# A graph network's first layer: every third block of nodes summed from rows gathered edge by edge

## What is computed

```python
h = jnp.maximum(_layernorm(x, axis=-1), 0.0)
msg = edge_val[:, None] * x[edge_src]          # x is h here, edge_val the edges' weights
neighbor = jax.ops.segment_sum(msg, edge_dst, num_segments=N_NODES)
out = neighbor @ W1.T + b1 + (x * neighbor) @ W2.T + b2
```

## Time and profile before

| | us |
|---|---|
| median of 3 runs | 2559.74 (2558.43 to 2564.2) |
| the profiled execution | 2558.8 |
| its span (first to last instruction) | 2556.4 |
| PE busy, and share of the span | 2265.3 (89%) |
| DVE busy | 1554.3 (61%) |
| ACT busy | 1235.4 (48%) |
| POOL busy | 133.9 (5%) |
| DMA, mean | 117 GB/s |

### The profile page before, as it was taken

The page is one execution under the profiler, slowest core; times in us unless marked ns, Lnnn a source line. Parts: engine busy times, 40 slices in busy tenths (PEclk is TensorE's granted clock), DMA queues, the critical chain, the costliest instruction groups (busy, mean ns, idle before and its releaser), DMA issues.

```text
span 2556.4 us, 58105 instructions
## 1 busy us (share of the span) xinstructions
PE 2265.3 (89%) x20263; PEld 2023.6 (79%) x20263; DVE 1554.3 (61%) x2760; ACT 1235.4 (48%) x3085; POOL 133.9 (5%) x114
## 2 busy tenths in 40 slices
PE   1599999999999999999987799999998426999897
PEld 1399999999999999999965566676787415888644
DVE  7677777777777777777745455555774582000133
ACT  4555555555555555555411577766886410000142
POOL 5300000000000000000000000000000340000000
PEclk7699999999999999999955899999999757999999
DMA  8222122112212212211233533233583147888221
GB/s 249 58 77 75 50 75 75 63 63 75 75 50 75 75 50 75 75 57 69 76 100 87 179 110 109 109 109 110 211 314 127 58 115 292 301 300 301 90 67 55
DMA packets 178788, 299.34 MB, mean 117 GB/s; under 512 B 13064, under 2 KB 130059, under 8 KB 178627
## 3 DMA queue, kind: packets, MB, share of 16 engines
q1 hardware_dynamic: 174592, 284.33, 32.2%
q0 software_dynamic: 4144, 14.34, 2.0%
HBM read 198.15 MB, written 100.49 MB: 117 GB/s over the span
## 4 chain that ended last, share of the span: by engine, by line
PE 82%; DVE 8%; DVEq 3%; issue 2%; ACT 2%; DMA 2%; ACTq 0%; POOLq 0%; POOL 0%; SPq 0%; PEldq 0%
PE ps L730 21%; PE ps L790 20%; PE ps L719 16%; PE ps L713 8%; PE ps L774 5%; PE ps L829 4%; PE ps L760 3%; PE ps L923 2%; DVE hT_s L1358 1%; DMA hs<-node_rows 1%; PE ps L820 1%; DVE carry L1554 1%; PE ps L837 1%; PE ps L960 0%; ACT edge_area L1010 0%
## 5 line engine op out<-in xcount | busy, mean ns | idle before, releaser
L1057 ACT CAST edge_area<-ps 128x392 f16<-128x392 f32 x784 | 385.5, 492 | 490.0 <-PE ps L713 490.0
L790 PE MATMUL ps<-big,rows_area 128*128 128x256 f16 (+1 forms) x4900 | 553.1, 274 | 24.8 <-DMA big<-edge_counts 24.8
L730 PE MATMUL ps<-big,rows_area 128*128 128x128 f32 x4802 | 571.3, 276 | 0.0
L730 PEld LDWEIGHTS ps<-big,rows_area 128*128 128x128 f32 x4802 | 550.9, 192 | 0.0
L719 PE MATMUL ps<-edge_area 128*128 128x196 f16 x4704 | 541.7, 250 | 0.0
L790 PEld LDWEIGHTS ps<-big,rows_area 128*128 128x128 f16 x4900 | 474.9, 99 | 82.8 <-DMA big<-edge_counts 25.1
L719 PEld LDWEIGHTS ps<-edge_area 128*128 128x128 f16 x4704 | 422.1, 97 | 0.3
L1063 ACT COPY big<-ps 128x392 f32<-128x392 f32 x784 | 384.5, 490 | 9.8 <-PE ps L719 1.4
L713 PE MATMUL ps<-edge_area 128*128 128x196 f16 x2352 | 334.4, 250 | 13.7 <-DVEq L1500 13.7
L1495 DVE TENSOR_TENSOR edge_area<-lo_pair,carry 128x768 f16<-128x768 f16 x392 | 218.7, 558 | 202.5 <-PE ps L719 124.1
L1496 DVE TENSOR_TENSOR edge_area<-cell_pair,carry 128x1176 f16<-128x1176 f16 x392 | 299.3, 764 | 0.0
(11 more groups left out here) (221 smaller groups left out, 1607.4 us busy)
## 6 DMA issues: line engine op xcount, KB each, us to landing
big<-edge_counts SPq DMA_DIRECT2D x336, 448.0 KB, 4.9
edge_counts<-edge_area SPq DMA_DIRECT2D x49, 1568.0 KB, 5.7
hs<-node_rows POOLq DMA_DIRECT2D x21, 448.0 KB, 4.5
x_stream<-edge_area SPq DMA_DIRECT2D x14, 448.0 KB, 3.9
node_rows<-edge_area SPq DMA_DIRECT2D x14, 448.0 KB, 3.0
edge_area<-x_stream SPq DMA_DIRECT2D x14, 448.0 KB, 3.9
node_rows<-rows_area SPq DMA_DIRECT2D x1, 3136.0 KB, 12.5
edge_area<-in_x SPq DMA_DIRECT2D x7, 448.0 KB, 4.7
```

What stands on the lines that cost most here:

```text
L730: last = mm(p_sum[par], h0[:, n, :], w32[:, par, n, :], start=(n == 0), stop=(n == NB - 1))
L790: last = mm(p_block[par][:, 0:width, :], planes[:, p, sh, :], piece[:, par, k, 0:width, j, :], start=(sh == 0 and p == 0), stop=(sh == NB ...
L1057: nc.scalar.copy(store_slot[:, par, :, cols], p_count[s % 2]).then_inc(sem("count_taken"), 1)
```

## The change

The halves are taken in sets of three (`SETS` = 16, and one half alone at the start). Of each set (in the code a `window(t)` with halves 3t+1, 3t+2 and 3t+3) two halves are done as before. The middle one, 3t+2, gets its counts but no weight matrix. Its sum is made edge by edge: its edges, at most 4608, lie as 36 columns (`SPAN`) of 128. For each column POOL gathers the 128 rows of h that the edges come from, from `node_rows` in HBM (64 KB), DVE makes an fp32 one-hot of the destination times the weight (`edge_onehots`), and PE multiplies the two, one fp32 matmul of 128x128 (`add_edges`), all 36 into one PSUM bank.

Three columns are a burst, and each set has 12 bursts: one is placed behind every fourth supergroup. Gathered rows have 12 buffers (`AHEAD` = 4 bursts), the one-hots 6 (`MADE` = 2 bursts). POOL also loads the next set's edge records (`load_set`), which DVE splits into indices and destinations (`split_set`, six small operations). The two remaining weight matrices' 98 matmuls are dealt over all 12 places, 8 or 9 each. The two PSUM banks of `weigh`'s sums become one for them and one for the edges. Loops now run over two sets on PE, ACT, DVE and POOL. A few small operations ahead of the stage work out where each set's records start; the general path for unsorted or too uneven input is taken too if a set has over 4608 edges.

```diff
+SETS = NHALF // 3
+SPAN = 36
+BURST = 3
+BURSTS = SPAN // BURST
+AHEAD = 4
+MADE = 2
...
+            def gather_set(t, q):
+                pool.wait_ge(sem("set_split"), t + 1)
+                for burst in range(BURSTS):
...
+                    pool.wait_ge(sem("edges_summed"), t * BURSTS + burst + 1)
...
+                    for n in range(BURST):
+                        c = burst * BURST + n
+                        pool.indirect_dma_start(
+                            out=edge_row[c % (AHEAD * BURST)], out_offset=None, in_=rows_dram,
+                            in_offset=bass.IndirectOffsetOnAxis(ap=set_idx[:, q, c:c + 1], axis=0),
+                        ).then_inc(sem(f"rows_in{burst % AHEAD}"), 16)
+                    if burst == AHEAD + 1:
...
+                        load_set(t + 1, 1 - q)
...
+            def add_edges(t, burst):
+                pe.wait_ge(sem(f"rows_in{burst % AHEAD}"), (t * (BURSTS // AHEAD) + burst // AHEAD + 1) * (16 * BURST))
...
+                pe.wait_ge(sem("edge_onehots"), t * BURSTS + burst + 1)
+                for n in range(BURST):
+                    c = burst * BURST + n
+                    last = mm(p_edges, edge_row[c % (AHEAD * BURST)], edge_oh[c % (MADE * BURST)],
+                              start=(c == 0), stop=(c == SPAN - 1))
+                last.then_inc(sem("edges_summed"), 1)
...
-            def duo_onehots(duo, slot):
-
-                dve.wait_ge(sem("weight_ready"), duo * 2 + 2)
+            def duo_onehots(duo, slot, weighted=True):
...
-                V.tensor_tensor(oh_whi[:, slot], oh_src[:, slot], whi.to_broadcast([P, 3, P, 2]), ALU.mult)
-                V.tensor_tensor(oh_wlo[:, slot], oh_src[:, slot], wlo.to_broadcast([P, 3, P, 2]), ALU.mult)
-                dve.drain()
+                if weighted:
+                    V.tensor_tensor(oh_whi[:, slot], oh_src[:, slot], whi.to_broadcast([P, 3, P, 2]), ALU.mult)
+                    V.tensor_tensor(oh_wlo[:, slot], oh_src[:, slot], wlo.to_broadcast([P, 3, P, 2]), ALU.mult)
+                    dve.drain()
                 dve.sem_inc(sem("onehots"), 1)
...
+            def edge_onehots(t, q, burst):
+                dve.wait_ge(sem("edges_summed"), t * BURSTS + burst + 1 + AHEAD - MADE)
+                for n in range(BURST):
+                    c = burst * BURST + n
+                    last = V.tensor_scalar(edge_oh[c % (MADE * BURST)], iota16[:, 0:P], set_dst[:, q, c:c + 1],
+                                           set_rec[:, q, c, 2:3], ALU.is_equal, ALU.mult)
+                last.then_inc(sem("edge_onehots"), 1)
...
+                for j in range(DUOS):
+                    if j < RING:
+                        slot_weighed(t * 2 + 2, j)
+                    else:
+                        slot_counted(t * 3 + 2, j)
+                    duo_onehots((t * 3 + 2) * DUOS + j, j % RING, weighted=False)
+                    if j % 2:
+                        edge_onehots(t, q, 4 + j // 2)
+                split_set(t + 1, 1 - q)
```

More of the change, by code:

```diff
@@ L525, in _ @@
                                     pattern=[[-1, P]], channel_multiplier=1).then_inc(sem("made"), 1)
+            pool.drain()
+            for j in range(4):
+                last = nc.gpsimd.tensor_copy(picker[:, j, :], ident[:, 32 * j:32 * j + 1].to_broadcast([P, P]))
+            last.then_inc(sem("made"), 1)
             for n, (first, last) in enumerate(TILES):
@@ L745, in count_sorted @@
                 pe.sem_inc(sem("weighed"), 2)
-                half(0, 0, False)
+                pe.sem_inc(sem("edges_summed"), AHEAD)
+                for s in range(SGS):
+                    supergroup(0, s, 0)
                 pe.wait_ge(sem("h0_ready"), 2)
-                with pe.Fori(0, NHALF // 2) as i:
-                    half(i * 2 + 1, 1)
-                    half(i * 2 + 2, 0)
-                weigh(NHALF - 1, 0, 0, NB)
+                with pe.Fori(0, SETS // 2) as i:
+                    window(i * 2)
+                    window(i * 2 + 1)
+                weigh(2 * SETS, 0, 0, NB, 3 * SETS)
             def multiply(l):
@@ L1508, in count_sorted @@
+            def count_sorted():
+                for j in range(DUOS):
+                    slot_weighed(0, j)
+                    duo_onehots(j, j % RING)
+                    if j == RING - 1:
+                        split_set(0, 0)
+                with dve.Fori(0, SETS // 2) as i:
+                    onehot_window(i * 2, 0)
+                    onehot_window(i * 2 + 1, 1)
                 dve.drain()
```

282 lines of the change are left out of this document (194 added, 88 removed).

## The result

| | median, us | lowest to highest | runs |
|---|---|---|---|
| before | 2561.0 | 2558.3 to 2564.2 | 7 |
| changed | 2574.2 | 2568.7 to 2589.8 | 7 |

The ratio is 1.0064 (95% interval 1.0038 to 1.0089): slower by 0.64%, where 1.1% faster was forecast (2533 us). The comparison was repeated three times beside the experiments, on three chips, with the unchanged code of both kernels. The experiments ran on five chips in all, e1 to e4 on the first and e5 to e8 on the second; which one the first comparison had is not known.

What follows compares the result with a forecast made beforehand. PE bounds the stage before, DVE after: 44.5 + 12.6 + 1.4 + 9.4 + 1.4 = 69.3 us per set. The stage then ends at 1253.6 instead of 1280.4, gaining 26.8 us: 2533 us, range 2447 to 2620.

Steps and rivals of the forecast that it cites:

- PE's prices: Supergroups at 0.79 us and fp32 matmuls at 0.225 us each; PE's need per set falls from 71.1 to 59.8 us.
- DVE becomes the bound: Per set DVE needs 67.9 us, 8.1 more than PE, so DVE's work sets the pace.
- The meetings with POOL: DVE's one-hots lose 0.24 us to POOL's transfers in every second burst: 1.4 us per set.
- Rivals 1 and 2: POOL becomes the bound: 2615 us, chance 0.17; DVE's one-hots wait for whole gathers: 2600 us, chance 0.10.
- rival 2: DVE's one-hots wait while a gather's issue holds the shared port, 5.6 us per set: 2600 us, chance 0.10.
- The stall in the long body: DVE's 482-row loop body might stall; seven stalls of 1.22 us, 9 us, considered but not charged in the forecast.
- rival 4: No change: port hits in every burst or long-body stalls make a set 70.5 to 71.3 us; 2559 us, chance 0.13.
- ACT and the middle half: PE's waits for ACT's copies in the unweighted half, at most 4.6 us a quarter, were costed at nothing.
- PE should not wait for rows: Four bursts of buffers, at least 14 us of PE's time, cover gather issue and landing, so no PE wait.
- The bound of 19 us: The most that PE's waits for ACT's copies in the middle half would cost over 16 sets, if uncovered.
- The clock at 1.00: PE's clock stays full although PE now waits in short gaps; nothing was charged for it.
- The load of x: Behind the stage, x's load would issue about 11 us after its end and stay hidden, 2 to 3 us left.

Runs made afterwards that it cites:

- e1: The changed kernel with the set loops of PE, DVE, ACT and POOL all written out: 2420.0 us, 0.947 of before.
- e4: The changed kernel with DVE's loop alone written out: 2457.9 us, 0.961 of before.
- e5: The changed kernel with all loops written out, but DVE's sets inside a loop of one pass: 2527.0 us, 0.986 of before.
- e8: The kernel before, given loop bodies as long as the changed kernel's: 2610.7 us, 1.0195 of before.
- e17: The changed kernel without gathers (twelve rows fetched once and multiplied in every set), on the fifth chip: 2526.2 us, 0.987 of before.
- e11: The kernel of e5 run again on the third chip: 2419.1 us, 0.946 of before.
- e9: The changed kernel, word for word, on the third chip: 2527.6 us, 0.988 of before.
- e16: The changed kernel, word for word, on the fifth chip: 2573.9 us, 1.0045 of before.
- e10: The kernel of e1 run again on the third chip: 2420.2 us, 0.947 of before.
- e15: The kernel of e1 with POOL's fetch of the next set's records two bursts earlier, on the fourth chip: 2424.1 us, 0.947 of before.
- e7: The kernel before with its three loops over the halves written out: 2561.3 us, 0.9996 of before.
- e18: The kernel of e15 run again on the fifth chip: 2505.1 us, 0.978 of before.

## Why the prediction was wrong

The sign was wrong on the upper chips, the first comparison's among them, and right on the lower ones; the time lay within the range on both. Two costs that the sum put at nothing made it wrong, and it took both: without the gathers an upper chip is at 2526 us (e17), with the loops written out at 2527 (e5), and both would have been faster than before. By its steps:

- **PE's prices: right, 2.6 us low.** 59.8 us were forecast as PE's need and 62.4 measured where it is the bound (e1). The quarters of the middle half are the difference: 4.15 us each (272.71 to 276.86 in e11), where the sum had 3.5, for PE waits 0.40 us for ACT there.
- **DVE becomes the bound: right**, by e9's 98 waits of PE for DVE's queue. The set inside a pass took 66.1 to 66.4 us for 69.3. A burst of one-hots takes 0.78 us, as forecast, but the issue gap that the sum had left behind the duo goes: about 0.15 us per burst, 1.8 per set. The meetings with POOL, 1.4 us, cost nothing that can be seen. The rows that answer to the earlier trace rows lie close to the forecast:

```profile
L1654 DVE TENSOR_SCALAR agg<-iota,clique_out,set_rec 128x128 f32<-128x128 f16 x252 | 72.6, 360 | 28.6 <-issue 14.9 <-remote 11.1 <-PE ps L811 2.7
```

```profile
L1152 ACT CAST edge_area<-ps 128x392 f16<-128x392 f32 x784 | 376.3, 491 | 484.8 <-PE ps L782 322.0
...
L628 POOL DMA_INDIRECT agg_s<-node_rows,shift x288 | 321.5, 1116 | 245.1 <-PE ps L811 154.0
L628 POOL DMA_INDIRECT hT_s<-node_rows,shift x288 | 352.7, 1225 | 147.6 <-issue 72.3
```

- **Rivals 1 and 2** (POOL as the bound; one-hots that wait for whole gathers) did not come: L1654 takes 0.36 us in the mean, a gather 1.12 to 1.23, and POOL still waits 154 us for PE. No one-hot waits for a whole gather, as rival 2 had it by the Trainium skill's rule on the locked pair of ports: L1654's longest are 0.56 us, where 0.45 is the longest without gathers (e17). What shows is the other way round: gathers, 0.94 us at the least, take up to 2.20.
- **The stall in the long body was mis-sized.** It stood in rival 4, with seven stalls of 1.22 us, 9 us in all, and in the forecast with nothing. Measured: 5.9 us for each of seven returns in e8, and 6.6 in e9 (72.9 less 66.4 us), 46 in all. The nearest row for it was of another kind: a pause in straight code and not a return to code that had gone. The body's growth from 38 to 482 rows stood in the text, and was not drawn to its end.
- The set forecast too long and the stall left out cancel. 16 sets at 3.0 us less are 48 us, seven returns 46. So on lower chips the kernel takes 2527 us for 2533, partly by luck: each step of the path that I had read well gained, and the one that I had not read took it back.
- **"ACT and the middle half ... I cost it at nothing" and "PE should not wait for rows" are the steps that failed by sign.** On upper chips the gathers bring stops, 47.7 us (e16 less e17), about half of them in that half (19 of e16's 38) and the others behind it and at the returns: the step is that of the gathers' cost beside PE and ACT, for which only DVE and POOL were looked at. PE does not wait for the rows, as forecast; it waits for ACT, which has PE's signal late. The bound of 19 us held ACT's copies alone; 48 were measured. No row of before holds a gather in this stage, and nothing in one trace shows that a cost depends on the chip.
- **The clock at 1.00** held on lower chips where DVE's loop was written out (e1, e4, e10, e11, e15). The window above has 0.96, e9's from 200 to 400 us 0.99: behind stops such as that of 5.03 us in e9 PE ran at half of it.
- **The load of x** was to stay hidden. Its issue follows the stage's end by 16.3 us in e9 and 20.3 in the first comparison, where 11 were forecast. What lies behind the stage takes 1276.0 us before, 1278.2 in e9, and 1288.2 in the first comparison's profiled execution, whose extra time is not the change's: it is 1288.6 in e7's, whose code there is that of before.

## What to carry to other kernels

When a change makes a loop body longer, compare each engine's body in instructions with what it was, and price one return to its head per pass, on the engine that sets the pace: here 4.6 to 5.7 us idle, and the clock behind it. Where DVE is the bound and its instructions are as short as 0.6 us, look at the "issue" between them: a loop's computed addresses took 0.3 us of each 2.8, and a written-out loop gave them back. Before believing a difference of 1 or 2% with its sign, run both kernels on more than one chip, above all when the change adds many small transfers.

## What the runs showed of the hardware

- A return to the head of a long body: DVE idle for 2.56 and again for 3.11 us (570 instructions, e9), PE for 4.64 us (1316, e8), ACT without an instruction for 5.6 us (356, first comparison). None on PE in 24 passes of a body of 440, where the branch takes 0.21 us and PE has no idle time.
- Written-out code of all four engines ran without any such pause (e1: PE never idle for over 1 us between 150 and 1130 us), though nothing of it is used twice; the instruction queues brought 103 and 62 packets there, 127 and 115 in the looped kernel.
- 128x128 one-hots times weight by two pointers, fp16 in and fp32 out: 0.36 us, and three in 0.86.
- On upper chips, with gathers, a sixth to a quarter of PE's recorded signals stand 0.3 to 5.3 us behind the recorded end of its work, ACT's and DVE's none (first comparison, e5, e16).
- Whether gathers stop PE depends on the chip, or on what came with it: two of the five had the stops (e5 to e8, e16 to e18), three had not. The changed kernel itself took 2574 us in both comparisons with stops and 2527 in both without.
